# Unread products in TensorE's waits of the second batch, and short norm operations moved from VectorE to GpSimd

## The reference

```python
x = L0_attn_x                                   # (8, 512, 128)
xn = (x - mean(x)) / sqrt(var(x) + 1e-5)
# attention
Q, K, V = (relu(xn @ W + b) for W, b in ((Wq, bq), (Wk, bk), (Wv, bv)))
scores = Qh @ Kh.T / sqrt(8), masked where sum(xn) == 0 and above the diagonal
out = softmax(scores) * query_mask @ Vh + xn
s = gamma * (out - mean) / sqrt(var + 1e-8) + beta
# feed-forward: 2 micro batches x 8 experts, expert e takes a fixed 256 tokens
n = (xn - mean(xn)) * rsqrt(var(xn) + 1e-5) * ln_scale + ln_bias
x_attn = n @ attn_w.T + attn_b + xn
h = gelu(x_attn @ w1[e] + b1[e]); eo = h @ w2[e] + b2[e]
g = silu(gelu(eo @ next_w.T + next_b))
return x + s * g
```

## Time and profile before

| what | value |
|---|---|
| median of three runs | 512.3 us (511.3 to 512.44) |
| the profiled execution, its own time | 512.2 us |
| its span in the trace | 510.4 us |
| mean granted TensorE clock over the span | 0.959 |
| busy: TensorE, weight loads, VectorE, ScalarE, GpSimd | 430.7, 267.3, 393.2, 301.9, 149.8 us |

### The profile page before, as it was taken

The page is one execution under the profiler, slowest core; times in us unless marked ns, Lnnn a source line. Parts: engine busy times, 40 slices in busy tenths (PEclk is TensorE's granted clock), DMA queues, the critical chain, the costliest instruction groups (busy, mean ns, idle before and its releaser), DMA issues.

```text
span 510.4 us, 10343 instructions
## 1 busy us (share of the span) xinstructions
PE 430.7 (84%) x3731; PEld 267.3 (52%) x3731; DVE 393.2 (77%) x968; ACT 301.9 (59%) x644; POOL 149.8 (29%) x367
## 2 busy tenths in 40 slices
PE   0039903999999899999999999999999999999880
PEld 0016702777777655555555555555555555555430
DVE  6989988888994297769769769778778778778507
ACT  0127603788888517666666666666666666666760
POOL 8000000000000221121471471471472372373293
PEclk9999955899999999999999999999999999999995
DMA  8900300344443302312322322222222232130000
GB/s 224 312 5 0 84 1 7 81 130 129 128 118 98 88 4 50 95 49 57 82 56 70 84 62 70 76 69 70 75 71 69 68 79 71 55 90 23 4 21 21
DMA packets 27513, 37.60 MB, mean 74 GB/s; under 512 B 5686, under 2 KB 19910, under 8 KB 27462
## 3 DMA queue, kind: packets, MB, share of 16 engines
q1 hardware_dynamic: 27302, 36.92, 26.0%
q0 software_dynamic: 160, 0.03, 0.0%
HBM read 25.91 MB, written 10.49 MB: 71 GB/s over the span
## 4 chain that ended last, share of the span: by engine, by line
PE 50%; DVE 9%; POOL 2%; issue 2%; ACT 1%; DVEq 0%; ACTq 0%; POOLq 0%
PE banks L988 14%; PE banks L1019 13%; PE banks L1007 11%; DVE mx L833 5%; PE banks L990 5%; PE banks L1009 5%; PE banks L1029 1%; DVE stats L880 1%; PE banks L1073 1%; DVE aggr L884 1%; ACT pt L954 1%; ACT ots L938 0%; DVE seed L71 0%; DVE bits L70 0%; PE banks L997 0%
## 5 line engine op out<-in xcount | busy, mean ns | idle before, releaser
L833 DVE TENSOR_REDUCE mx<-banks 128x1 f32<-128x384 f32 (+3 forms) x384 | 210.1, 596 | 63.4 <-PE banks L990 58.0
L954 ACT ACTIVATE pt<-banks 128x512 f32<-128x512 f32 (+2 forms) x384 | 184.5, 527 | 101.9 <-PE banks L1009 90.5
L990 PE MATMUL banks<-causal,ident_b 128*128 128x128 bf16 x512 | 102.8, 220 | 0.0
L1009 PE MATMUL banks<-causalT,ident_b 128*128 128x128 bf16 x512 | 102.3, 219 | 0.0
L1019 PE MATMUL banks<-pt,vg 128*18 128x512 f32 (+3 forms) x1024 | 81.4, 436 | 1.3 <-ACT pt L954 1.3
L988 PE MATMUL banks<-w_room 73*128 73x512 bf16 (+3 forms) x256 | 69.0, 302 | 3.4 <-DVE mx L833 3.4
L988 PE MATMUL banks<-k_own,q_own 73*128 73x512 bf16 (+3 forms) x256 | 69.2, 302 | 3.0 <-DVE mx L833 2.5
L1007 PE MATMUL banks<-w_room 76*128 76x512 bf16 (+3 forms) x256 | 67.7, 300 | 1.5 <-ACT pt L954 1.5
L1007 PE MATMUL banks<-q_own,k_own 76*128 76x512 bf16 (+3 forms) x256 | 68.5, 300 | 0.2 <-ACT pt L954 0.2
L733 POOL TENSOR_SCALAR mneg<-mx 128x16 f32<-128x16 f32 x32 | 8.1, 255 | 168.1 <-DVEq L841 168.1
L990 PEld LDWEIGHTS banks<-causal,ident_b 128*128 128x128 bf16 x512 | 50.1, 98 | 0.9
(11 more groups left out here) (162 smaller groups left out, 635.1 us busy)
## 6 DMA issues: line engine op xcount, KB each, us to landing
k_scratch<-parts SPq DMA_DIRECT2D x40, 128.0 KB, 2.4
q_own<-q_scratch SPq DMA_DIRECT2D x48, 96.0 KB
k_own<-k_scratch SPq DMA_DIRECT2D x48, 96.0 KB
w_room<-q_scratch SPq DMA_DIRECT2D x48, 96.0 KB
w_room<-k_scratch SPq DMA_DIRECT2D x48, 96.0 KB
q_scratch<-parts SPq DMA_DIRECT2D x24, 128.0 KB, 2.4
w_room<-in_w_dram SPq DMA_DIRECT2D x1, 2048.0 KB, 9.6
out_dram<-mixed SPq DMA_DIRECT2D x7, 256.0 KB, 2.3
```

Of the source, the lines that this page charges most:

```text
L833: ins = dve.tensor_reduce(mx[:, u % 2, heads[0]:heads[-1] + 1, q], banks[:, S0 + c % RING, 0:w * len(heads)].rearrange("p (h k) -> p h k", ...
L954: act.activation(weights(k, heads[0], len(heads)), banks[:, ST0 + j % RING, 0:(T - P * k) * len(heads)], ACT.Exp, scale=SCALE).then_inc(ex ...
L990: ins = mm(o[:, w - P:w], ident_b[:, :], causal[:, :], start=False, stop=True)
L1009: ins = mm(o[:, 0:P], ident_b[:, :], causalT[:, :], start=False, stop=True)
```

## The change

It has four parts, all in stage one.

1. The twelve Newton operations of `second_roots`, for each of the two groups, go from VectorE to GpSimd (`second_seeds` on VectorE keeps six operations and raises `seeds_ready`). Of `sums(i)` VectorE keeps the wide reduction alone, without a wait behind it, and raises `lanes_ready`; GpSimd's new `totals(i)` does six short operations and raises `sums_ready`. The copy of the root is gone, since ScalarE reads root and shift where they lie. The mask is made once at the end (`masks`), in three operations, behind all eight `sums_ready`.
2. In VectorE's order `second_seeds` and `rests(1)` of group 1's opening stand before `quotients(2)`; `rests(1)` stood behind it.
3. In batch 0 the projections Q, K and V stand before the transposes of the second norm and `attn_product(0)` on TensorE, and `split(0)`, which takes them out, before `second_norm(0)` on ScalarE.
4. TensorE makes 28 unread products between the two halves of the second expert products of batch 1 and 40 behind them (`hold`).

```diff
+HELD = (28, 40)
...
+                def second_roots(tok, group):
+
+                    at = slice(group[0], group[0] + group[1])
+                    pool.wait_ge(seeds_ready, tok.next(seeds_ready))
+                    for _ in range(3):
+                        link(tt(t2[:, at], y2[:, at], y2[:, at], ALU.mult))
+                        link(tt(t2[:, at], t2[:, at], v2[:, at], ALU.mult))
+                        link(pool.tensor_scalar(t2[:, at], t2[:, at], -0.5, 1.5, ALU.mult, ALU.add))
+                        link(tt(y2[:, at], y2[:, at], t2[:, at], ALU.mult))
+
+                def totals(tok, i):
+
+                    at = slice(TB * i, TB * i + TB)
+                    pool.wait_ge(lanes_ready, tok.next(lanes_ready))
...
+                    link(pool.tensor_scalar(shift[:, at], rem[:, at], -1.0 / C, None, ALU.mult))
+                    link(tt(shift[:, at], shift[:, at], y2[:, at], ALU.mult))
+                    pool.sem_inc(sums_ready, 1)
...
                 def sums(i):
 
                     tiles = slice(TB * i, TB * i + TB)
-                    row_sum(link, dve, rem[:, tiles], s16[:, tiles, :], s8[:, tiles, :, :], s4[:, tiles, :],
-                            s2[:, tiles, :], xn_all[:, tiles, :])
-                    link(dve.scalar_tensor_tensor(out=norm2[:, i, 1], in0=rem[:, tiles], scalar=-1.0 / C,
-                                                  in1=y2[:, tiles], op0=ALU.mult, op1=ALU.mult))
-                    link(dve.tensor_copy(norm2[:, i, 0], y2[:, tiles]))
-                    dve.sem_inc(sums_ready, 1)
-                    link(dve.tensor_scalar(zero_all[:, tiles], rem[:, tiles], 0.0, None, ALU.is_equal))
+                    dve.tensor_reduce(s16[:, tiles, :], xn_all[:, tiles, :].rearrange("p n (k l) -> p n l k", l=16),
+                                      AX.X, ALU.add).then_inc(lanes_ready, 1)
...
                 roots(GROUPS[1])
+                second_seeds(GROUPS[1])
+                rests(tok, 1)
                 for i in range(2, B):
                     quotients(i)
-                    rests(tok, i - 1)
-                    if i == 2:
-                        second_roots(GROUPS[1])
+                    if i > 2:
+                        rests(tok, i - 1)
                     sums(i)
-                    if i == B - 1:
-                        link(dve.tensor_scalar(live_all[:, :], zero_all[:, :], -1.0, 1.0, ALU.mult, ALU.add))
-                        dve.tensor_scalar(mask_b[:, :], zero_all[:, :], -BIG, None, ALU.mult).then_inc(mask_ready, 1)
                     lows(tok, i - 1)
+                masks()
...
+                def hold(n):
+
+                    for _ in range(n):
+                        mm(banks[:, TRX, :], ones_p[:, :], bias_rows[:, 0:1, :].broadcast_to([P, TB, C]),
+                           start=True, stop=True)
...
                     for h in range(2):
+                        if i == 1 and h == 1:
+                            hold(HELD[0])
                         pe.wait_ge(hid_ready, tok.next(hid_ready))
...
                     ins.then_inc(eo_done, 1)
+                    if i == 1:
+                        hold(HELD[1])
```

More of the change, by code:

```diff
@@ L193, in build_program @@
         xl_st = s1("xl_st", [P, 2, TB, C])
-        norm2 = s1("norm2", [P, B, 2, TB])
+        shift = s1("shift", [P, NT])
         xnT = s1("xnT", [P, 2, T])
@@ L229, in build_program @@
             "mask_ready", "maskT_done", "maskT_ready", "mask_out"))
-        mean, var, a, y, t, s, sh, sl, r, nr, rem, v2, y2 = (small[:, k, :] for k in range(13))
+        mean, var, a, y, t, s, sh, sl, r, nr, rem, v2, y2, t2 = (small[:, k, :] for k in range(14))
         with nc.Block() as block:
@@ L387, in quotients, with second_seeds @@
                     dve.sem_inc(xn_ready, 1)
-                def second_roots(group):
+                def second_seeds(group):
                     at = slice(group[0], group[0] + group[1])
@@ L428, in _ @@
                 quotients(0)
-                second_roots(GROUPS[0])
+                second_seeds(GROUPS[0])
                 sums(0)
@@ L490, in gelu_out, with split @@
                         product_out(tok)
-                tok = Tokens(act)
-                norm_out(tok, 0)
-                second_norm(tok, 0)
-                second_out(tok)
-                product_out(tok)
-                for i in range(B):
-                    n, last = i % STEPS, i == B - 1
+                def split(tok, i):
                     for o, bias, done in ((0, bq, q_done), (1, bk, k_done)):
@@ L510, in _ @@
                                    ACT.Relu).then_inc(vb_free, 1)
+                tok = Tokens(act)
+                norm_out(tok, 0)
+                split(tok, 0)
+                second_norm(tok, 0)
+                second_out(tok)
+                product_out(tok)
+                for i in range(B):
+                    n, last = i % STEPS, i == B - 1
+                    if i > 0:
+                        split(tok, i)
                     if last:
@@ L593, in _, with attn_product, bias_first, next_product @@
                     ins.then_inc(v_done, 1)
+                def attn_product(tok, n):
+                    pe.wait_ge(xlT_ready, tok.next(xlT_ready))
+                    mm(banks[:, XB, :], wattn_sb[:, :], xlT[:, :], start=True, stop=False)
+                    if n > 0:
+                        pe.wait_ge(xnT_ready, tok.next(xnT_ready))
+                    mm(banks[:, XB, :], ident[:, :], xnT[:, n % 2, :], start=False, stop=True).then_inc(xa_done, 1)
+                def bias_first(row):
+                    return mm(banks[:, VB, :], ones_p[:, :],
+                              bias_rows[:, row:row + 1, :].broadcast_to([P, TB, C]), start=True, stop=False)
+                def hold(n):
+                    for _ in range(n):
+                        mm(banks[:, TRX, :], ones_p[:, :], bias_rows[:, 0:1, :].broadcast_to([P, TB, C]),
+                           start=True, stop=True)
+                def next_product():
+                    pe.wait_ge(eoT_ready, tok.next(eoT_ready))
+                    bias_first(1).then_inc(w2_done, 1)
+                    for k in range(TB):
+                        ins = mm(banks[:, VB, P * k:P * k + P], eoT[:, P * k:P * k + P], wnext_sb[:, :],
+                                 start=False, stop=(k == TB - 1))
+                    ins.then_inc(next_done, 1)
+                tok = Tokens(pe)
+                normed(tok, 0)
+                pe.wait_ge(xnT_ready, tok.next(xnT_ready))
+                projections(tok, 0)
+                second_normed(tok, 0)
+                attn_product(tok, 0)
+                for i in range(B):
+                    n = i % STEPS
+                    if i > 0:
+                        projections(tok, i)
                     if i == B - 1:
@@ L623, in _ @@
                         attn_product(tok, i + 1)
-                for _ in range(IDLE_PRODUCTS):
-                    mm(banks[:, TRX, :], ones_p[:, :], bias_rows[:, 0:1, :].broadcast_to([P, TB, C]),
-                       start=True, stop=True)
+                hold(IDLE_PRODUCTS)
     with ExitStack() as two:
```

50 lines of the change are left out of this document (26 added, 24 removed).

## The result

The changed kernel takes 506.27 us (median of four runs, 504.82 to 506.85), against 512.37 us (511.3 to 512.44) before: a ratio of 0.988, 95% interval 0.986 to 0.991. It is faster by 6.1 us. The profiled execution had 506.25 us with a span of 504.5 us, so it lies where the median lies.

The account below looks back on a forecast made before the run. VectorE was taken as the bound up to 88.4 us, where batch 2 opens, TensorE from there. Terms of 2.6 and 2.2 us sum to 4.8, from 512.2 to 507.4, median 507.5 us; range 502.5 to 511.8.

Parts of the forecast that it names:

- VectorE to the sums of batch 1: With short operations off VectorE, means of group 1 could start 5.6 us earlier, at 39.4 instead of 45.01 us.
- Batch 0: With projections first on TensorE and ScalarE, first hid at 45.0 us and variances of group 1 3.5 us earlier.
- Quotients of batch 2: On VectorE, quotients(2) starts at 70.3 us, takes 7.9 plus 0.6 us for GpSimd's Newton operations; reduction ends at 79.85.
- Totals of batch 2: GpSimd's six operations of totals(2), each waiting for VectorE's running operation, take 4.2 us; xl_st starts 2.6 us earlier.
- Clock: Unread products in batch 1's waits let batch 2 open at the high clock on TensorE, saving 2.2 us.
- The products cost nothing in themselves: The unread products in batch 1 add no time, since both TensorE waits they stand in are longer.
- B: Rival: the clock is low when batch 2 opens, 2.2 us stay lost, 2.6 us gained, 509.7 us; chance 0.14.
- Sum: Whole kernel: 2.6 + 2.2 = 4.8 us gained, 512.2 to 507.4 us, median of three 507.5.
- A: Rival: GpSimd is not held up, totals(2) takes 1.7 us, 7.9 us gained in all, 504.4 us; chance 0.24.
- C: Rival: GpSimd is shut out for whole VectorE runs, its eighteen early operations end at 39.6 us; 514 us, chance 0.11.
- The rest: Mask operations and totals(3) and later change nothing; they run in VectorE's waits and TensorE's 13.66 us cover the totals.

Follow-up runs that it names:

- e8: The changed kernel with 38 unread products ahead of the transposes of batch 0 and 16 behind its projections: 503.42 us, ratio 0.984.
- e6: The changed kernel with one unread reduction of 1280 columns on VectorE behind the reduction of batch 2, ahead of lows(1): 504.27 us, ratio 0.986.
- e1: The changed kernel without the 68 unread products: 507.63 us, ratio 0.991 to the kernel before.
- e2: The changed kernel with no unread products in batch 1's first wait and 40 in the second: 506.19 us, ratio 0.989.
- e11: The changed kernel as it is, timed once more: 505.9 us, ratio 0.990.
- e3: The kernel before with unread products alone, 80 in batch 1's first wait and 18 in the second: 510.88 us, ratio 0.998.
- e7: The changed kernel with the short operations of sums(2) on VectorE, all other batches' on GpSimd: 506.0 us, ratio 0.988.
- e9: e8 with the totals of batches 2, 3 and 4 on VectorE and 44 and 34 unread products in batch 1's waits: 503.13 us, ratio 0.984.
- e12: e9 with the totals of all batches from 2 on on VectorE: 502.15 us, ratio 0.982.

## Why the prediction was right, and where it was off

The forecast of 507.5 us was 1.2 us too high, the case the likeliest one.

- **VectorE to the sums of batch 1:** `means` of group 1 at 39.4 us predicted, 39.52 found.
- **Batch 0:** xl_st(0) at 35.0 predicted and 34.58 found, the first `hid` 45.0 and 44.75. But `variances` came 2.8 us earlier, not 3.5. The term that was too small is "`hid` to the end of the second bf16 part was 4.07 us": at the low clock the first `hid` operations wait for their products, and it took 5.04 us (44.75 to 49.14 + 0.65). e8, with the high clock there, won those and more.
- **Quotients of batch 2:** 70.3 predicted, 71.29 found, 0.7 of the lateness from the step above. The twelve Newton operations were to cost VectorE 0.6 us; from its first quotient to the reduction it took 7.97 us, where the earlier trace rows has 7.90 for the quotients, and from `rests(1)` to the operation behind it 1.75 instead of 1.68, so they cost 0.14. GpSimd did the waiting: up to 0.77 us for an operation beside VectorE's 0.69.
- **Totals of batch 2:** 4.2 us predicted, 3.27 found from the reduction's end to xl_st. The mechanism was right (e6), the size not: I let all six wait, and the second and third slipped into the idle 0.5 us between the operations of `lows(1)` (the rows at 81.05 and 81.35). The Trainium skill (SBUF — State Buffer, Who interferes with whom) says that `tensor_reduce` never contends; 1.7 us for the six beside a reduction and 3.03 beside two-input operations agree.
- **Clock:** 2.2 us predicted, 2.39 found in the trace, 1.4 by the medians of e1. The products ended at 83.16 us, inside the 81.9 to 84.5 I gave, 2.08 us ahead of the transposes, and the clock held. "The products cost nothing in themselves" holds for this execution alone: in e2 and e11 they kept the transposes back by 0.4 and 0.7 us. And the 2.5 us between the last product and the fall, which I took from one row as the mark for B, don't decide: the clock held through the wait of 2.72 us here and fell after 2.1 us in e11 (67.80 to 69.90).
- **Sum:** 2.6 + 2.2 predicted, 3.15 + 2.39 found, and 0.4 us in stage two that no step has. That the first term came so near is partly luck. `quotients(2)` began 1.0 us later than forecast; from there VectorE took 0.6 us less to the end of the reduction, and the totals 0.9 less. These errors nearly cancel.
- **Rivals:** A (GpSimd not held up) fell with the 0.77 us rows; e6 shows what it would have been. B (low clock) is e1's case, 2.62 us in the trace, and did not come. C (shut out for whole runs) fell at 31.39 us: beside runs of four unlinked operations GpSimd's follow each other every 0.28 to 0.33 us, nearly as if alone, and the run of 1.14 us takes at most 1.19. The eighteen operations ended at 34.5 us, not at 38.
- **The rest:** "TensorE's 13.66 us cover them" holds for the changed kernel (5.54 us at batch 2 and at batch 7). e3, e7 and e9 show how little cover that is: any gain ahead of batch 2 beyond it goes in the next batch with a longer way.

The parts don't add up. Taken away one by one they cost 1.4 (products), 4.6 (order of batch 0) and 3.6 us (Newton operations), 9.6 in all (by the ratios 1.6, 5.2 and 3.6), where the whole brings 6.1; products added alone (e3) bring Q of batch 2 forward by 2.4 us and the whole by 0.9.

## What to carry to other kernels

Before a wait at the start of a pipeline is shortened, compare the periods of the engines behind it: where the second is within a few per cent of the first (14.0 against 13.66 us here), the gain comes back as a wait a batch later. Short operations are cheap to give to GpSimd where their result is wanted late, as with the Newton steps, and dear where somebody waits for them beside two-input work of VectorE, as with the totals. And a long wait in front of a critical stretch is worth filling with unread products only as far as its end: 40 of the 68 did all of it, and where the low clock slowed them they ran past it.

## What the runs showed that I had not expected

- VectorE hardly pays for GpSimd's short operations: 0.14 us for twelve beside `rests(1)` and the quotients, and at most 0.05 us on a run of 1.14 us.
- Beside a run of unlinked SCALAR_TENSOR_TENSOR operations of 128 columns, whose operands lie in SBUF too, GpSimd's operations are hardly held up (0.20 to 0.30 us each, one 0.39), beside one TENSOR_TENSOR of 512 columns they are (up to 0.77 us for 0.69). By the Trainium skill (SBUF — State Buffer, Who interferes with whom) a VectorE instruction with two SBUF inputs contends with a GpSimd one that reads SBUF; for these short ones the rows hardly show it, and the measurement decides. Which of length and form makes the difference was not tried.
- The clock in batch 0 differs between executions of nearly the same list: `variances` came between 47.97 (e6) and 50.86 us (e2), and in e11 at 48.88, so one profiled execution settles no difference of 2 us there. With products ahead (e8, e9, e12) it came at 47.67 to 47.81 us in all three.
